# Counting over a trial threshold: from VectorE's compares to ScalarE's accumulated signs, in three overlapped batches

## The reference, cut to what matters

```
sim = einsum('bhnd,bhmd->bnm', Q, K) / (sqrt(d) * H)      # per batch 512 x 512
k = int(512 * 0.3)                                         # 153
threshold = top_k(sim, k)[0][:, :, -1:]                    # the 153rd largest of each row
A = sigmoid(sim) * (sim >= threshold)
A = (A + swapaxes(A, -1, -2)) * 0.5
x = x + tanh(g) * ((1 - gamma) * layernorm(x) + gamma * A)
```

## Time and profile before

| What | us |
|---|---|
| median of three runs | 1830.92 |
| the profiled execution, its own time | 1819.78 |
| its span | 1818.0 |
| PE busy | 1500.6 (83%) |
| DVE (VectorE) busy | 1314.6 (72%) |
| ACT (ScalarE) busy | 737.9 (41%) |
| POOL (GpSimd) busy | 468.5 (26%) |

### The profile page before, as it was taken

How to read it: one execution, slowest core, us unless ns; L and a number is a source line. 1 busy time by engine, 2 the same in 40 slices (tenths; PEclk the granted TensorE clock), 3 DMA queues, 4 the chain that set the end, 5 groups by cost and what they waited for, 6 DMA issues and landing times.

```text
span 1818.0 us, 24191 instructions
## 1 busy us (share of the span) xinstructions
PE 1500.6 (83%) x8186; PEld 722.2 (40%) x8186; DVE 1314.6 (72%) x2448; ACT 737.9 (41%) x1060; POOL 468.5 (26%) x438
## 2 busy tenths in 40 slices
PE   3277687964889988168888988898899999999998
PEld 1144444532555555012223222222354444444544
DVE  6887868556999995888878878785655555556555
ACT  5353536223444444216656656567122222222222
POOL 4211212102666664610000000000223333233232
PEclk8589898986999999559999999999999999999999
DMA  5211212113555553634210300213400000000000
GB/s 166 83 31 60 65 56 60 66 54 104 163 174 179 174 170 117 170 84 74 41 27 2 53 6 14 40 24 80 83 1 0 23 0 0 23 0 0 23 12 12
DMA packets 115031, 114.29 MB, mean 63 GB/s; under 512 B 59448, under 2 KB 87352, under 8 KB 114944
## 3 DMA queue, kind: packets, MB, share of 16 engines
q1 hardware_dynamic: 109184, 94.29, 18.6%
q0 software_dynamic: 5760, 18.88, 3.8%
HBM read 59.53 MB, written 31.46 MB: 50 GB/s over the span
## 4 chain that ended last, share of the span: by engine, by line
PE 57%; DVE 30%; issue 5%; DMA 4%; ACT 3%; POOL 1%; SPq 1%; DVEq 0%; ACTq 0%; POOLq 0%
PE PS L1928 17%; PE PS L1951 9%; PE PS L829 7%; PE PS L1403 6%; DVE WORK L1528 6%; PE PS L1382 5%; PE PS L1391 3%; PE PS L844 3%; DVE WORK L1770 2%; DVE WORK L1788 2%; DVE WORK L1771 2%; PE PS L1941 1%; DVE WORK L1762 1%; DMA WORK<-in_L_ffn_down_w_dram 1%; DVE X L1472 1%
## 5 line engine op out<-in xcount | busy, mean ns | idle before, releaser
L1528 DVE TENSOR_REDUCE WORK<-PS 128x1 f32<-128x512 f32 x512 | 325.9, 685 | 69.2 <-PE PS L1382 68.3
L1928 PE MATMUL PS<-BIG 128*128 128x512 f16 x1536 | 339.2, 381 | 8.3 <-DVE BIG L2006 4.6
L1310 ACT ACTIVATE BIG<-PS 128x1024 f32<-128x1024 f32 x256 | 261.5, 1024 | 161.8 <-PE PS L1391 160.6
L1382 PE MATMUL PS<-BIG 128*128 128x512 f16 x512 | 205.4, 403 | 65.7 <-DVE WORK L1528 42.7
L1928 PEld LDWEIGHTS PS<-BIG 128*128 128x128 f16 x1536 | 150.7, 98 | 188.2 <-DVE BIG L2006 7.0
L829 PE MATMUL PS<-BIG,WORK 128*128 (+1 forms) x1152 | 182.2, 315 | 4.8 <-DVE WORK L864 4.8
L1951 PE MATMUL PS<-BIG 128*128 128x512 f16 x768 | 173.8, 379 | 1.8 <-DVE BIG L2026 1.8
L1864 ACT ACTIVATE WORK<-PS 128x512 f32<-128x512 f32 x64 | 38.2, 597 | 303.1 <-PE PS L1928 303.1
L1391 PE MATMUL PS<-BIG 128*128 128x512 f16 x512 | 154.7, 386 | 0.1
L1403 PE MATMUL PS<-BIG 128*32 128x512 f32 x1024 | 138.8, 614 | 9.9 <-issue 6.9
L1382 PEld LDWEIGHTS PS<-BIG 128*128 128x128 f16 x512 | 50.0, 98 | 243.7 <-DVE WORK L1528 197.3
(11 more groups left out here) (244 smaller groups left out, 2277.5 us busy)
## 6 DMA issues: line engine op xcount, KB each, us to landing
wdq_scratch<-WORK SPq DMA_DIRECT2D x48, 256.0 KB
WORK<-in_L_ffn_w_dram SPq DMA_DIRECT2D x32, 352.0 KB, 3.5
y_scratch<-WORK SPq DMA_DIRECT2D x40, 256.0 KB, 2.8
BIG<-BIG SPq DMA_DIRECT2D x96, 64.0 KB, 2.3
X<-in_x_dram SPq DMA_DIRECT2D x4, 1024.0 KB, 9.1
WORK<-in_L_ffn_w_dram SPq DMA_DIRECT2D x16, 256.0 KB, 2.9
WORK<-in_L_ffn_gate_w_dram SPq DMA_DIRECT2D x16, 256.0 KB, 3.5
WORK<-in_L_ffn_up_w_dram SPq DMA_DIRECT2D x16, 256.0 KB, 3.6
```

Source lines behind the costliest of these rows:

```text
L1310: nc.scalar.activation(PB[:, tp, 2 * h:2 * h + 2, :], BPAIR[h % 2], ACT.Exp, scale=SOFT_SCALE).then_inc(exp_ok, 1)
L1382: nc.tensor.matmul(ABANK[i], QS[:, g * HG + h, r * P:(r + 1) * P], KA[:, g, :], start=True, stop=True).then_inc(a_mm, 1)
L1528: v.tensor_reduce(MXU[:, g % 2, c:c + 1], ABANK[i], AX_X, ALU.max, negate=True).then_inc(max_ok, 1)
L1928: ins = nc.tensor.matmul(bank[b], fxT[:, p, a, k * P:(k + 1) * P], w[:, c, l, k, :], start=(i == 0), stop=(i == 3 * KD - 1))
```

## The change

In the three overlapped batches (b = 1, 2, 3) `search_step` is no longer called. ScalarE runs `counts(b, n)` instead: for each of the 4 row tiles an activation Sign of (th_try - sim) over 128 x 512, with the sum of the signs accumulated into the count. The sum is 512 minus twice the number over the threshold, so the factors of the small instructions change with it (-0.5 and S / 2 - AIM; the difference of two counts is halved). The signs themselves go to a scratch tile `signs` in the place of `topw`. VectorE runs `search_counted(b, n)`, which has the small instructions only. Two semaphores tie them: `th_ok` (VectorE: the trial threshold is set) and `cnt_ok` (ScalarE: a row tile is counted). From its third activation on, ScalarE also waits until the activation two before has finished, since they share a half of `signs`.

In ScalarE's order `counts(b, 0)` stands ahead of the `act_hi` of the batch's first tile, and `counts(b, 1)` and `counts(b, 2)` stand right behind the `act_sil` of i = 1 and i = 2. In VectorE's order `dve_lo` of the first tile comes straight after `search_start`; `search_counted(b, 0)`, `(b, 1)` and `(b, 2)` stand behind the `half` of u = 0, 1 and 2. Batch 0 keeps `search_step`.

```diff
+        signs = carve(WORK, "signs", 20480, [P, 2, S], F16)
...
+            def counts(b, n):
+                act.wait_ge(th_ok, (b - 1) * TRIES + (n + 1))
+                count = count0 if n % 2 == 0 else count1
+                for r in range(R):
+                    done = ((b - 1) * TRIES + n) * R + r
+                    if done >= 2:
+                        act.wait_ge(cnt_ok, done - 1)
+                    nc.scalar.activation(signs[:, r % 2, :], sim[:, r, :], ACT.Sign, bias=th_try[:, r:r + 1], scale=-1.0,
+                                         accum_out=count[:, r:r + 1]).then_inc(cnt_ok, 1)
...
                     act_thi(act, SH, NEAR, 1, 2 * t0 - 1)
+                counts(b, 0)
                 act_hi(act, SH, NEAR, t0 % 2, t0)
...
                     act_sil(act, SH, NEAR, h, u, 0)
+                    if 1 <= i < TRIES:
+                        counts(b, i)
...
-                link(v.scalar_tensor_tensor(th_try, row_dev, 0.52, smv[:, :, 0], ALU.mult, ALU.add))
+                ins = v.scalar_tensor_tensor(th_try, row_dev, 0.52, smv[:, :, 0], ALU.mult, ALU.add)
+                if b:
+                    ins.then_inc(th_ok, 1)
+                else:
+                    link(ins)
...
+            def search_counted(b, n):
+
+                count, last = (count0, count1) if n % 2 == 0 else (count1, count0)
+                dve.wait_ge(cnt_ok, ((b - 1) * TRIES + (n + 1)) * R)
+                dve.wait_ge(th_ok, (b - 1) * TRIES + (n + 1))
+                if n:
+                    link(v.tensor_tensor(diff, count, last, ALU.subtract))
+                    link(v.scalar_tensor_tensor(diff, diff, -1.0, diff, ALU.mult, ALU.max))
+                    link(v.tensor_scalar(diff, diff, 0.5, 1.0, ALU.mult, ALU.max))
+                    link(v.reciprocal(diff, diff))
+                    link(v.scalar_tensor_tensor(step, step, -1.0, step, ALU.mult, ALU.max))
+                    link(v.tensor_tensor(gain, step, diff, ALU.mult))
+                link(v.tensor_scalar(outside, count, -0.5, S / 2.0 - AIM, ALU.mult, ALU.add))
+                link(v.tensor_tensor(step, outside, gain, ALU.mult))
+                link(v.tensor_tensor(outside, outside, outside, ALU.mult))
+                link(v.tensor_scalar(outside, outside, WINDOW ** 2 / 4.0, None, ALU.is_gt))
+                link(v.tensor_tensor(step, step, outside, ALU.mult))
+                ins = v.tensor_tensor(th_try, th_try, step, ALU.add)
+                if n + 1 < TRIES:
+                    ins.then_inc(th_ok, 1)
+                else:
+                    link(ins)
...
                 search_start(b)
                 dve_lo(dve, SH, NEAR, t0 % 2, t0)
-                search_step(0)
                 half(u, t0, 0)
-                search_step(1)
+                search_counted(b, 0)
                 half(u + 1, t0, 0)
-                search_step(2)
+                search_counted(b, 1)
                 half(u + 2, t0, 0)
+                search_counted(b, 2)
                 window((0, 1))
```

More of the change, by code:

```diff
@@ L147, in build @@
         sig_sb = sem("sig_sb")
+        th_ok = sem("th_ok")
+        cnt_ok = sem("cnt_ok")
         xmix = sem("xmix")
```

## The result

| | before | after |
|---|---|---|
| median of the runs, us | 1829.89 (1826.46 to 1832.27, 4 runs) | 1854.07 (1851.57 to 1856.66, 4 runs) |
| the profiled execution | 1819.78 | 1854.66 |
| its span | 1818.0 | 1852.9 |
| L553 of batch 1 to L1041, the overlapped stage | 299.7 | 326.5 |

The ratio is 1.0136 (95% interval 1.0119 to 1.0153): 24.2 us slower, against 31.6 forecast. The two profiled executions lie 34.9 us apart, in part because that of before is one of its fastest runs.

What follows compares the result with a forecast made beforehand. In the overlapped batches' front halves, waits alternate among PE, ScalarE and VectorE, with one of three steps' counts on the path. Delays of 9.7 + 12.7 + 9.2 = 31.6 us on 1830.9 gave about 1862, range 1846 to 1876.

Steps and rivals of the forecast that it cites:

- The place of group 0: Front half: counts(b, 0) ahead of the first tile's copy makes PE's first multiply and everything behind it start 3.6 us later.
- what would show it: Signs expected in the trace after, among them VectorE's first subtraction about 4.3 us behind the end of L553, not 0.24.
- The price of a group: ScalarE: four Sign activations with accumulated output take 3.2 us, between 2.5 and 4.0; each 0.1 us moves the forecast 0.9.
- The fronts' sum: First threshold guess to window, three overlapped batches: later by 9.7 + 12.7 + 9.2 = 31.6 us.
- No table of its own for Sign: ScalarE: Sign needs no load; the rival, nine loads adding 11.5 us (1874), had chance 0.07.
- ScalarE as the later one ahead of silu of u = 2: Front half, batch 1: ScalarE's tables, sigmoids and chunks end at 122.6, while PE's multiply would be ready about 119.7.
- the staged chunk's wait in batch 2: ScalarE's 4.46 us idle for a staged load stays but comes later, so window starts 12.7 us later in batch 2.
- VectorE's work as the bound: Rival: window starts 8.9 us earlier in each batch, 26.8 faster, 1804; chance 0.06 including a smaller form.
- "All of it kept" in the back half: From window to the next batch nothing starts earlier, so the whole 31.6 us delay stays.
- a sign of being wrong: The distance from window to the next batch shrinks; the prediction expected that length unchanged.
- The total: Whole kernel: 31.6 us slower, about 1862 us; 1856 to 1870 for the forecast itself, chance 0.77.
- the absorbed case: Rival: back-half idle time takes half to all of each batch's delay, leaving 0 to 16 us, 1831 to 1847; chance 0.10.

Runs made afterwards that it cites:

- the second profile of before: The kernel before, unchanged, profiled again: one execution at 1828.35 us, span 1826.6, overlapped stage 303.8 us.
- the twelve profiles: All profiles of the study together: five of kernels whose counts all run on VectorE, seven with any count on ScalarE; no single time.
- the experiment on the copy: The kernel after, with counts(b, 0) moved behind the act_hi copy of the first tile: ratio to before 1.0085, 1843.71 against 1827.25 us.
- the sigmoids' move: Four sigmoids of each batch moved to the end of i = 3: ratio 1.0011 on the kernel before, 1.0075 on the kernel after (both to before).

## Why the prediction was right, and where it missed

**The place of group 0** held. VectorE's first subtraction starts 3.55 us behind the end of L569 instead of 0.24 (forecast: 3.8), with 3.47 of idle ahead of it, and the hidden product is 3.3 us later (11.04 against 7.78 behind the first guess; forecast 3.6). In what would show it I wrote 4.3 us, which my own timetable (97.7 less 93.86) does not give.

**The price of a group** was too high: 3.2 taken, 2.83 measured (95.09 to 97.92). The readout starts before its activation has ended (95.72 against 95.81) and the next activation starts 0.09 behind the readout's start, so one comes every 0.70 to 0.72 us. Where a table load follows, as behind group 1, it waits for the end of the readout, and the group costs 2.94 (113.08 to 116.02). The row alone, 2.93 for four, would have been closer. Over nine groups that is some 3.1 us. From the formula of the Trainium skill, "ScalarE: Activation LUTs", section What ACT_TABLE_LOAD costs, an activation with a bias pointer over 512 elements is an estimate of 706 ns, and the trace agrees with 710 (mean of 36). With that section's overlap of 93 ns the next would come after 0.61 us, again an estimate; the trace has 0.70, with the readout, which the section doesn't price, in between.

**The fronts' sum was right by luck.** The 3.1 us were made good by something for which the sum had no term. In each batch one small instruction of step 2 took 1.0 to 1.3 us more than its 0.16, 3.5 us in all: L611 at 130.01, and

```profile
225.74 1.44 DVE L611 TENSOR_TENSOR WORK<-WORK 128x4 f32<-128x4 f32 x1
...
316.76 1.15 DVE L609 TENSOR_TENSOR WORK<-WORK 128x4 f32<-128x4 f32 x1
```

each beside a subtraction of GpSimd; that of batch 1:

```profile
129.90 1.52 POOL L258 TENSOR_TENSOR BIG<-WORK,BIG 128x704 f16<-128x704 f32 x1 [6.84 <-ACT BIG L241]
```

The trace of before had shown such instructions: I priced the 12 at 2.4 us from the earlier trace rows, a step in which none was slowed, while steps 1 and 2 of batch 1 each have one like this:

```profile
106.79 1.33 DVE L562 TENSOR_TENSOR WORK<-WORK 128x4 f32<-128x4 f32 x1
```

**No table of its own for Sign** held: the rows around L349 show a silu and a sigmoid load where they were and none in front of a group. The Trainium skill's rule ("ScalarE: Activation LUTs", section Table sets: the hidden batching unit) that cheap functions are in every set agrees with these rows if Sign is one of them; its list there does not name it. On the other cost of a table, the load at 114.52, which I had named for it, has 2.40 us of idle time behind it, a wait for PE; the better row is the load at 106.90, 1.28 us, with silu at 108.20.

**ScalarE as the later one ahead of silu of u = 2** held in all three batches, and the staged chunk's wait in batch 2 was 4.45 against the 4.46 put into the sum. Moving group 0 behind the copy, the sigmoids, or the sigmoids and all counts confirms it: less on ScalarE's stretch takes the time away, in the front halves to within 2 us a batch of the timetable.

**VectorE's work as the bound** fell: 36 counts fewer, 28.0 us of VectorE's busy time less, and slower. With step 0 alone moved, 12 counts less left the fronts within 0.2 us of the second profile of before.

**"All of it kept" in the back half** was the step that failed. Batches 1 and 2 gave back 2.9 and 2.4 us between `window` and the next first guess. I had named that as a sign of being wrong, and to this size I was. Two small things account for it, neither of them the idle time of the earlier trace rows: its two waits in the back halves are 4.60 and 4.92 us before, 4.61 and 4.92 after. In batch 1 before, VectorE's L593 met GpSimd's subtraction of the last chunk. VectorE's row, and L581's, of before:

```profile
129.98 0.97 DVE L581 SCALAR_TENSOR_TENSOR WORK<-WORK 128x512 f32<-128x512 f32 x1
...
137.93 1.20 DVE L593 TENSOR_TENSOR WORK<-WORK 128x64 f32<-128x64 f32 x1
```

GpSimd's row of before:

```profile
137.90 1.15 POOL L255 TENSOR_TENSOR BIG<-WORK,BIG 96x512 f16<-96x512 f32 x1 [7.50 <-ACT BIG L238]
```

After, `window` being later, both have gone free of it:

```profile
140.87 0.69 DVE L624 SCALAR_TENSOR_TENSOR WORK<-WORK 128x512 f32<-128x512 f32 x1
...
148.54 0.23 DVE L636 TENSOR_TENSOR WORK<-WORK 128x64 f32<-128x64 f32 x1
```

That is 1.25 us. And PE's product behind it, 3.63 us at 140.32 in the earlier trace rows at a mean granted clock of 0.56, now ran at 1.00, the higher level (2.4 GHz). PE had stood still for less time ahead of it (1.34 us instead of 2.31, and 0.75 instead of 1.81 one wait earlier):

```profile
148.44 0.18 PE L437 MATMUL PS<-WORK,ONES 128*128 128x4 f16 x1 [0.75 <-DVE WORK L633]
149.95 2.10 PE L887 MATMUL PS<-BIG 128*128 128x512 f16 x9 [1.34 <-DVE X L683]
```

That is 1.53 us more; 2.78 of the 2.94 together. In batch 2 the wait of 2.30 became 1.34 and the product of 3.62 us 2.10, which is 2.5 against the 2.4 given back. Both are read from traces, no experiment isolated them. That this product runs at either level shows in batch 3 too, with the idle time ahead of it. The first profile of before:

```profile
308.28 0.18 PE L421 MATMUL PS<-WORK,ONES 128*128 128x4 f16 x1 [1.53 <-DVE WORK L590]
309.79 2.10 PE L844 MATMUL PS<-BIG 128*128 128x512 f16 x9 [1.33 <-DVE X L640]
```

and the second, where VectorE was 2.5 us later by the two slowed instructions shown above, and the granted clock was 0.50, the lower level (1.2 GHz):

```profile
312.33 0.18 PE L421 MATMUL PS<-WORK,ONES 128*128 128x4 f16 x1 [4.00 <-DVE WORK L590]
313.84 4.00 PE L844 MATMUL PS<-BIG 128*128 128x512 f16 x9 [1.34 <-DVE X L640]
```

The product takes 1.9 us more there; with the 2.5 that is 4.4 of the 5.4 by which the two differ behind `window` in that batch, and most of the rest is in PE's next multiply. In the twelve profiles this product stands 36 times. All 23 with 1.79 us or more of idle time ahead of the small product L421 took 3.4 to 4.0 us, and 11 with 0.34 to 1.53 took 2.10. But two in the experiment on the copy, with 1.15 and 1.48, took 2.73 and 3.38, so this idle time alone does not settle the level.

**The total**: 31.6 forecast for the stage; 31.2 less 4.4 is 26.8 by the first profile, 22.6 by the second; 24.2 timed (21.8 to 28.0). The time, 1854.07, lies 2 us under the 1856 to 1870 that I gave the forecast itself, and inside the whole range only because that reached down for the absorbed case. Direction and mechanism held. The term that failed is the back half's nothing, and the scatter of the stage had no term at all.

## What to carry to other kernels

An engine with a low busy share still has stretches in which others wait for it, and new work belongs where it idles, not where the program text is convenient: the same 36 activations made this kernel 24 us slower or 15 us faster. Write the timetable of the one stretch, instruction by instruction on every engine; it gave each batch's delay to 0.3 us, though with two errors of about 1 us a batch that cancelled. Look there also for small instructions that run beside another engine's work: here they cost 1.0 to 1.3 us apiece and moved with every edit. And when a move fails, look for what can leave the crowded stretch with it: the sigmoids' move was worth nothing alone and 1.2% beside the counts.

## What the runs showed of the hardware that I had not expected

- The readout of ScalarE's accumulator is an instruction of its own, of 0.19 us, but costs the flow only about 0.09 us: activations of 0.71 us with it come every 0.70 us, while two of 0.62 us without it take 1.15 together, which is an overlap of 0.09.
- VectorE's 128x4 instructions take 0.16 to 0.18 us, but 66 of them in the overlapped stages of the twelve profiles took 0.3 to 1.5 us, and every one of these ended within 0.15 us of the end of a GpSimd subtraction (130.01 to 131.44 beside 129.90 to 131.42). One over 128x512 went from 0.69 to 1.97 us in the same way, while a MAX8 at 301.44 kept its 0.70 beside GpSimd's 301.25 to 302.79.
- One and the same product of PE took 2.10 or 4.00 us in two executions of one program, at a granted clock of 1.00 or 0.50, with 1.5 or 4.0 us of standing still ahead of the instruction before it.
- Unchanged later stages were up to 8 us longer behind some edits (the second attention stage 461.0 to 464.7 us with counts on ScalarE, 458.9 to 459.9 without; the passage 13.2 to 16.4 and 13.1 to 14.5). 72 and 24 empty instructions did not bring it about in the attention stage. It sets a floor of some 0.4% under what a profile of the changed stretch can say of the total here.
